# First experts' results stored by slot and gathered back in pairs of row tiles, in batch order; second experts' weights loaded between those stores

## The chip, the cores and the metric

The kernel runs on one core of a Trainium2 chip. The metric is the device time of one execution in microseconds (us). TensorE does the matmuls and transposes, VectorE and ScalarE the element-wise work and the copies out of PSUM, GpSimd (POOL in the profile) some element-wise work and all indirect DMAs, and SyncE (SP) only issues DMAs.

## The reference

An embedding of 8 batches, each of 64 image patches and 128 text tokens, so 8 x 192 = 1536 rows of 192 numbers, goes through two layers. Only the last three steps bear on the change:

```python
h = h + L0_ffn(layernorm(h))   # 8 experts, top 2, hidden 288, gelu
h = h + L1_attn(layernorm(h))
h = h + L1_ffn(layernorm(h))   # 8 experts, top 2, hidden 768, silu; output
# L1_attn: linear attention, 12 heads of 16, per batch:
k_, q_ = relu(k) + 0.25, relu(q) + 0.25
kv, k_sum = sum_n k_[n] v[n]^T, sum_n k_[n]
out = ((q_ kv) / (q_ k_sum + 1e-6)) @ proj_w.T + proj_b
```

In L0_ffn a row's result is the sum of two experts' results, each times its gate.

## The kernel before

**Tiles.** The 1536 rows are 12 row tiles of 128. Tiles 0 to 3 hold the patches of two batches each, tiles 4 to 11 the text of one batch each. The two batches of index i are `trio(i)`: patch tile i and text tiles 4 + 2i and 5 + 2i. There are four trios, and six pairs of neighbouring tiles.

**Experts.** A routing step ranks the 2 x 1536 (row, expert) entries by expert, so that each expert's rows fill whole tiles of 128 slots: 31 tiles in all. `slot` numbers are kept per entry (`sli`), and per slot the row to fetch (`idxs`) and the place of the result (`idx2`). `expert_dma` (L731) is GpSimd's program. It gathers tile i + 7's rows by an indirect DMA (L738), into a ring of 4 buffers, then stores tile i's result by another (L746). `experts` (TensorE L1903, VectorE L1529, ScalarE L1019) transposes a gathered tile, makes the hidden layer (L1941), transposes it, makes the result (L1983), and VectorE copies it (`evac_y`, L1571) into a ring of 8 buffers. The first experts' results go to `ybuf` in HBM: one row for each (choice, row), and spare rows for slots without an entry.

**Sum.** When all stores have landed, `load_acc` (L545) reads `ybuf` back with plain DMAs, the first choices' results on SP's queue into `xn`, the second choices' on ScalarE's into `a1`, each in four groups of row tiles (`ACC`). SP then issues the second experts' weights, 9.2 MB. VectorE adds each group into `h`, times the gate, and takes its statistics (`ln_start`, `ln_end`). ScalarE normalises (`ln_norm`, L834).

**Attention.** TensorE transposes the rows by neighbouring pairs (`t_pair`, L1839). `kv_mms` (L2218) makes keys and values of two pairs in four PSUM banks, `q_mms` (L2247) the queries of two pairs, `sums` (L2270) the key-value sums of a trio, `numden` (L2293) its numerators and denominators, `t_att` (L2322) and `out_proj` (L2330) the projected result. VectorE copies keys (L1642) and queries (L1650) out, masks the sums (`state`), divides (`ratio`, L1678), and adds the result to `h` (`add_att`). ScalarE copies the transposed rows (L1088), the values (L1098) and the transposed attention (L1118). Each engine's order is written out by hand. `keep_busy` (L1799) puts matmuls whose result nobody reads into a wait.

After it come the second routing and the second experts, whose results GpSimd adds into `out`.

Of the kernel before, what the change touches and what calls it, by code (L numbers as in the profile page):

```python
# [28 lines left out]
ALU = mybir.AluOpType  # L29
# [36 lines left out]
YRING = 8  # L66
NV = 2
# [23 lines left out]
LANDED = [16 * (sum(1 for n in range(NT) if n % YRING == (i - 1) % YRING) + (i - 1) // YRING + 1) if i else 16  # L91
# [7 lines left out]
def build(nc, x, out):  # L99
    ctx = ExitStack()  # L100
    with ctx:
# [26 lines left out]
        ybuf = nc.dram_tensor("expert_rows", [TOPK * NTOK + 32 * P, D], F32, kind="Internal").ap()  # L128
# [213 lines left out]

        psum = ctx.enter_context(nc.psum_tensor("bank", [P, 8 * 512], F32))
# [37 lines left out]
        route_done = sem("route_done"); idx2_ready = sem("idx2_ready"); land_ready = sem("land_ready"); turn_come = sem("turn_come")  # L381
# [5 lines left out]
        acc_ld = [sem(f"acc_ld{g}") for g in range(4)]  # L387
# [10 lines left out]
        NPAIR = NJ // 2  # L398
        NBP = B // 2
# [21 lines left out]
        PR_BANK = [(4, 7), (4, 7), (4, 7), (0, 1)]  # L421
# [32 lines left out]
        def ln_cols(n, g):  # L454
            if n == 3:
                return slice(*ACC[g])
# [96 lines left out]


        @block.sync
        def _(sp):
# [49 lines left out]
            load_acc(sp, 0)  # L606

            for e in range(NE):
# [9 lines left out]
            sp.wait_ge(xn5_ready, NJ)  # L618
            sp.dma_start(tok_rows(xd[1][:, 0:D]), xn[:, :, :]).then_inc(xd_written, 16)
# [1859 lines left out]
```

## Time and profile before

| | |
|---|---|
| time, median of 3 runs | 462.23 us (457.75 to 463.28) |
| profiled execution: its time | 462.79 us |
| profiled execution: its span | 461.0 us |
| mean granted TensorE clock | 0.956 of full speed |
| busy share of the span: TensorE matmul | 91% |
| weight load (PEld) | 71% |
| VectorE | 63% |
| GpSimd | 49% |
| ScalarE | 43% |

The span runs from the first to the last instruction that the profile shows of the core, and the execution's time is 1.8 us more. A busy share is a mean over stages that have different limits. Times in rows are us from the start of the span. "<-" before a name is what released the engine from the wait.

### The profile page before, as it was taken

Reading aid. Unit: us, or ns where it says so; the run is one execution under the profiler, and the core shown is the slowest. Engines: PE = TensorE matmul, PEld = TensorE weight load, DVE = VectorE, ACT = ScalarE, POOL = GpSimd, SP = SyncE. Lnnn points to the kernel's source line nnn. Section 1 sums busy time; section 2 is a strip of 40 time slices with the busy share of each in tenths; the row PEclk is TensorE's granted clock in tenths of the full one; section 3 lists DMA queues with packets and bytes.
Section 4 is the critical chain, followed back from the end, with each engine's and each line's share of the span. In section 5 each row is a group of like instructions: output and inputs, shape, how many; then the busy total and the mean of one; then the engine's idle time right before and its main releaser. Section 6 shows DMA issues by size and latency. Waiting matters only on the chain.

```text
span 461.0 us, 10231 instructions
## 1 busy us (share of the span) xinstructions
PE 420.2 (91%) x3568; PEld 326.3 (71%) x3568; DVE 292.3 (63%) x1360; ACT 197.3 (43%) x374; POOL 225.6 (49%) x266
## 2 busy tenths in 40 slices
PE   7999998989788988989987988977999999999993
PEld 5653655637536877878844557933999999999993
DVE  6579999999782433333558336887465566556651
ACT  1287945441751111110123401546566566566660
POOL 4302798797035666666520000334456665665544
PEclk9799799999989999898979999998999999999998
DMA  8609400010132122222169999079233233333322
GB/s 233 96 1 227 113 0 3 1 35 1 58 102 70 60 61 70 69 70 70 47 195 236 224 225 217 15 137 139 50 62 50 54 62 63 51 55 61 51 25 27
DMA packets 40128, 39.02 MB, mean 85 GB/s; under 512 B 7575, under 2 KB 37259, under 8 KB 40079
## 3 DMA queue, kind: packets, MB, share of 16 engines
q1 hardware_dynamic: 28861, 23.05, 22.5%
q0 software_dynamic: 9312, 14.03, 15.3%
q10 hardware_dynamic: 1906, 1.30, 1.0%
q8 instruction: 29, 0.48, 0.4%
q14 instruction: 20, 0.16, 0.1%
HBM read 28.00 MB, written 11.06 MB: 85 GB/s over the span
## 4 chain that ended last, share of the span: by engine, by line
PE 66%; DVE 11%; DMA 10%; ACT 4%; POOL 4%; issue 4%; POOLq 1%; SPq 0%; DVEq 0%; another core or an unknown queue 0%; ACTq 0%
PE bank L1955 11%; PE bank L1990 10%; PE bank L1941 7%; PE bank L1983 7%; DMA out<-a,idx 5%; PE bank L2036 4%; POOL reg L707 3%; PE bank L1803 3%; PE bank L1964 2%; DMA xn<-expert_rows 2%; PE bank L1918 2%; ACT xn L834 2%; DMA reg<-xn_rows,idxs 1%; PE bank L2229 1%; DMA reg<-in_patchT 1%
## 5 line engine op out<-in xcount | busy, mean ns | idle before, releaser
L738 POOL DMA_INDIRECT reg<-xn_rows,idxs x62 | 60.5, 976 | 30.3 <-issue 16.6
L1955 PE MATMUL bank<-reg,xT 64*128 64x128 f32 x1116 | 72.6, 275 | 1.4 <-issue 1.1
L758 POOL DMA_INDIRECT out<-a,idx x31 | 50.3, 1622 | 46.7 <-DMA out<-a,idx 35.8
L1955 PEld LDWEIGHTS bank<-reg,xT 64*128 64x128 f32 x1116 | 68.6, 188 | 1.5 <-issue 1.0
L1990 PE MATMUL bank<-reg 64*128 64x192 f32 x744 | 69.0, 323 | 0.0
L1990 PEld LDWEIGHTS bank<-reg 64*128 64x128 f32 x744 | 63.4, 187 | 0.0
L1803 PE MATMUL bank<-con 128*128 128x512 bf16 x201 | 55.3, 435 | 0.0
L1045 ACT ACTIVATE reg<-reg 128x1152 f32 x31 | 36.1, 1163 | 30.8 <-PE bank L1990 30.8
L1574 DVE TENSOR_SCALAR a<-bank,gs 128x192 f32<-128x192 f32 x31 | 13.0, 418 | 53.2 <-PE bank L1990 53.2
L1024 ACT ACTIVATE reg<-bank 128x288 f32<-128x288 f32 x31 | 12.5, 410 | 77.4 <-PE bank L1941 62.9
L746 POOL DMA_INDIRECT expert_rows<-a,idx x31 | 30.6, 986 | 25.2 <-DVE a L1571 19.1
L1803 PEld LDWEIGHTS bank<-con 128*128 128x128 bf16 x201 | 21.6, 111 | 27.6 <-issue 12.0
L1941 PE MATMUL bank<-reg,xTs 96*128 (+1 forms) x124 | 36.7, 418 | 4.8 <-DVE xTs L1537 4.7
L1983 PE MATMUL bank<-reg 96*128 x186 | 36.9, 336 | 0.3 <-issue 0.3
L1571 DVE COPY a<-bank 128x192 f32<-128x192 f32 x31 | 11.0, 354 | 39.6 <-PE bank L1983 20.6
L1983 PEld LDWEIGHTS bank<-reg 96*128 96x128 f32 x186 | 32.8, 195 | 3.7 <-issue 0.8
L1547 DVE TENSOR_SCALAR reg<-bank,gb 128x128 f32<-128x128 f32 x93 | 32.3, 403 | 0.0
L787 POOL TENSOR_SCALAR onep<-rs 128x3 f32<-128x3 f32 x4 | 0.9, 228 | 57.2 <-DVE nm L1189 57.2
L1941 PEld LDWEIGHTS bank<-reg,xTs 96*128 96x128 f32 (+1 forms) x124 | 21.8, 196 | 9.8 <-issue 6.2
L707 POOL TENSOR_TENSOR reg<-reg 128x128 f32<-128x128 f32 x63 | 26.1, 457 | 5.1 <-PE bank L2110 4.9
L1028 ACT ACTIVATE reg<-bank 128x384 f32<-128x384 f32 x31 | 15.2, 490 | 21.7 <-PE bank L1955 13.4
L1309 DVE TENSOR_REDUCE bank<-reg 128x6 f32<-128x24 f32 x176 | 23.9, 181 | 0.0
(363 smaller groups left out, 800.9 us busy)
## 6 DMA issues: line engine op xcount, KB each, us to landing
reg<-in_w2b SPq DMA_DIRECT2D x8, 576.0 KB, 10.2
reg<-in_w1b SPq DMA_DIRECT2D x8, 288.0 KB, 10.4
reg<-in_w1a SPq DMA_DIRECT2D x8, 216.0 KB
reg<-in_w2a SPq DMA_DIRECT2D x8, 216.0 KB
xn_rows<-xn SPq DMA_DIRECT2D x4, 384.0 KB, 2.7
reg<-in_w1b SPq DMA_DIRECT2D x8, 192.0 KB, 8.5
xn_rows<-xn SPq DMA_DIRECT2D x1, 1152.0 KB, 7.8
out<-h SPq DMA_DIRECT2D x1, 1152.0 KB
```

The costliest lines, as they stand in the source:

```text
L707: ins = nc.gpsimd.tensor_tensor(term[b % 2][k][:, 0:n, :, r, :], second[:, :, :, r, k:k + 1].to_broadcast([P, n, NCH, 4]), first[:, :, :, ...
L738: pool.indirect_dma_start(xs[:, i % RING, 0:(D, D2)[l]], None, xd[l], bass.IndirectOffsetOnAxis(ap=idxs[:, i:i + 1], axis=0)).then_inc(xs_ ...
L746: pool.indirect_dma_start(ybuf, bass.IndirectOffsetOnAxis(ap=idx2[:, i:i + 1], axis=0), ys[:, i % YRING, :], None).then_inc(scat[i % YRING ...
L758: pool.indirect_dma_start(out, bass.IndirectOffsetOnAxis(ap=idx2[:, i:i + 1], axis=0), ys[:, i % YRING, :], None, compute_op=ALU.add).then ...
L1045: nc.scalar.activation(w2r[:, p, :], w2b.rearrange("p e c n -> p (e c n)")[:, bass.ds(e * W2R, W2R)], ACT.Copy).then_inc(w2r_act, 1)
L1309: V.tensor_reduce(slot(t)[:, ch, 0:3], entries[:, ch], AX, ALU.add).then_inc(scan_self[half], 1)
L1547: ins = V.tensor_scalar(dst[:, k], src[:, :, 64 * k:64 * k + 64], gb2[:, 0, k:k + 1], gb2[:, 1, k:k + 1], ALU.mult, ALU.add)
L1803: MM(bank[bk][:, :], con[:, 0:P // 2].bitcast(BF16), con[:, 0:2 * P].bitcast(BF16), start=True, stop=True)
L1941: ins = MM(bank[2 + p][:, 0:hid], xTs[0:r, p, k, :], w1v[0:r, bass.ds(e * (NK * hid) + k * hid, hid)], start=(k == 0), stop=(k == NK - 1))
L1955: ins = MM(bank[2 + 2 * p + a][:, c * P:(c + 1) * P], w1r[rs, p, col:col + hc], xT64[rs, p, k, :], start=(c == 0 and k == 0), stop=(c == n ...
L1983: ins = MM(bank[6 + p][:, 0:D], hTs[0:r, p, c * P:(c + 1) * P], w2v[0:r, bass.ds(e * (nhc * D) + c * D, D)], start=(c == 0), stop=(c == nh ...
L1990: ins = MM(bank[Y_BANKS[i == NT - 1][a]][:, 0:D], hT2[rs, p, c * P:(c + 1) * P], w2r[rs, p, c * D:(c + 1) * D], start=(c == 0), stop=(c == ...
```

## The change

The first experts' result of tile i is stored by a plain DMA of SP, in slot order: row 128 i + p of `ybuf` is slot p of tile i. GpSimd only gathers in that stage (`first_dma`). Between those stores SP loads the second experts' weights, one expert after every third tile from tile 3 on. When all stores have landed, GpSimd fetches each row's two results by `sli`: 24 indirect gathers of 128 rows (`results_back`), by pairs of row tiles in batch order (`ORDER`: patch tile and two text tiles of each trio). VectorE adds and normalises by such pairs (`rows_back`), and `h`, `xn`, keys, values and queries are handled by pairs in that order, on every engine. The keys and values of one pair have two PSUM banks in place of four for two pairs, and queries are made for two, two, one and one pairs. The rows for the second gather are written by 12 DMAs in place of 2. The diff, cut to its core (a "..." line stands where lines are left out):

```diff
+SCAT0 = NA // YRING
...
-        ybuf = nc.dram_tensor("expert_rows", [TOPK * NTOK + 32 * P, D], F32, kind="Internal").ap()
+        ybuf = nc.dram_tensor("expert_rows", [NT * P, D], F32, kind="Internal").ap()
...
-        PR_BANK = [(4, 7), (4, 7), (4, 7), (0, 1)]
+        ND_BANK = [(6, 7), (6, 7), (6, 7), (2, 3)]
+        PR_BANK = [(6, 7), (6, 7), (6, 7), (4, 5)]
...
-        ACC = ((0, 2), (2, 4), (4, 8), (8, 12))
-        GROUPS[3] = [list(range(*ab)) for ab in ACC]
-        LN_BASE = {1: 0, 2: 3, 3: 5, 4: 5 + len(ACC)}
+        ORDER = [j for i in range(NBP) for j in trio(i)]
+        GROUPS[3] = [ORDER[2 * n:2 * n + 2] for n in range(NPAIR)]
...
-        def wait_scatters(eng, l):
+        def wait_results(eng, done):
             for s in range(YRING):
-                eng.wait_ge(scat[s], 16 * (sum(1 for i in range(NT) if i % YRING == s) * (l + 1)))
-        def load_acc(eng, p):
-            wait_scatters(eng, 0)
-            buf = (xn, a1)[p]
-            rows = tok_rows(ybuf, p * NTOK)
-            for g, ab in enumerate(ACC):
-                js = slice(*ab)
-                eng.dma_start(buf[:, js, :], rows[:, js, :]).then_inc(acc_ld[g], 16)
+                eng.wait_ge(done[s], 16 * (sum(1 for i in range(NT) if i % YRING == s) + (0 if done is y_st else SCAT0)))
         @block.sync
...
-            load_acc(sp, 0)
-            for e in range(NE):
+            def load_expert(e):
...
                 sp.dma_start(w2b[:, e, :, :], x["w2b"][e].rearrange("(c p) n -> p c n", p=HC1)).then_inc(ld_ffn1, 16)
+            for i in range(NT):
+                sp.wait_ge(y_ev, i + 1)
+                sp.dma_start(ybuf[i * P:(i + 1) * P, :], ys[:, i % YRING, :]).then_inc(y_st[i % YRING], 16)
+                if 3 <= i < 27 and i % 3 == 0:
+                    load_expert(i // 3 - 1)
...
+            for i0, i1 in ((0, NBP - 1), (NBP - 1, NBP)):
+                sp.wait_ge(xn5_ready, 3 * i1)
+                of = xn[:, 3 * i0:3 * i1, :].rearrange("p (i v) n -> p i v n", v=3)
+                pat = slice(i0, i1)
+                for c, n in ((slice(0, D), D), (slice(D, DX), DX - D)):
+                    sp.dma_start(tok_rows(xd[1])[:, pat, c], of[:, :, 0, 0:n]).then_inc(xd_written, 16)
+                    for a in range(2):
+                        sp.dma_start(tok_rows(xd[1])[:, NPJ + 2 * i0 + a:NPJ + 2 * i1:2, c],
+                                     of[:, :, 1 + a, 0:n]).then_inc(xd_written, 16)
...
+            def first_dma():
+                rows_written(0)
+                for i in range(NT):
+                    gather(0, i)
+            def results_back(n):
+                for q in (2 * n, 2 * n + 1):
+                    for k, buf in enumerate((xn, a1)):
+                        a, g = k * NJ + ORDER[q], 2 * q + k
+                        if g >= YRING:
+                            pool.wait_ge(scat[g % YRING], 16 * (g // YRING))
+                        pool.indirect_dma_start(buf[:, q, :], None, ybuf,
+                                                bass.IndirectOffsetOnAxis(ap=sli[:, 0, a:a + 1], axis=0)
+                                                ).then_inc(scat[g % YRING], 16)
...
             route_share(0)
-            expert_dma(0)
-            wait_scatters(pool, 0)
+            first_dma()
+            wait_results(pool, y_st)
+            results_back(0)
             link(nc.gpsimd.memset(vb[:, :, KC:KV], 1.0))
+            results_back(1)
             nc.gpsimd.memset(attT[KC:KC + 1, 1, :], 1.0).then_inc(att_ones, 1)
+            for n in range(2, NPAIR):
+                results_back(n)
...
-                    nc.scalar.activation(xn[:, j, :], src[:, j, :], ACT.Identity,
+                    nc.scalar.activation(xn[:, i, :], src[:, j, :], ACT.Identity,
...
-            for q in range(2):
-                ln_std(3, q)
-                ln_norm(3, q, h)
-                xt3_evac(q)
-            for g in range(1, 3):
-                ln_std(3, g + 1)
-                ln_norm(3, g + 1, h)
-                v_evac(g - 1)
-                xt3_evac(2 * g)
-                xt3_evac(2 * g + 1)
...
+            def rows3(n):
+                ln_norm(3, n, h)
+                xt3_evac(n)
...
+            ln_std(3, 0)
+            rows3(0)
+            ln_std(3, 1)
+            v_evac(0)
+            rows3(1)
+            ln_std(3, 2)
+            v_evac(1)
+            rows3(2)
+            ln_std(3, 3)
             v_evac(2)
...
+            rows3(3)
+            ln_std(3, 4)
+            v_evac(3)
             att_evac(0)
+            rows3(4)
+            ln_std(3, 5)
+            v_evac(4)
+            rows3(5)
             att_evac(1)
             ln_std(4, 0)
             norm5(0)
...
-                        dve.wait_ge(scat[s], 16 * turns(l, i, YRING))
+                        dve.wait_ge((y_st, scat)[l][s], 16 * (turns(0, i, YRING) + l * SCAT0))
...
-            for g, ab in enumerate(ACC):
-                dve.wait_ge(acc_ld[g], 16 * 2)
+            def rows_back(n):
+                for g in range(4 * n, 4 * n + 4):
+                    dve.wait_ge(scat[g % YRING], 16 * (g // YRING + 1))
                 for k, y in ((0, xn), (1, a1)):
-                    for j in range(*ab):
-                        ins = V.scalar_tensor_tensor(out=h[:, j, :], in0=y[:, j, :], scalar=gate[:, k, j:j + 1],
+                    for q in (2 * n, 2 * n + 1):
+                        j = ORDER[q]
+                        ins = V.scalar_tensor_tensor(out=h[:, j, :], in0=y[:, q, :], scalar=gate[:, k, j:j + 1],
                                                      in1=h[:, j, :], op0=ALU.mult, op1=ALU.add)
...
+            def q_evac(c):
+                first, r = Q_PAIRS[c]
+                dve.wait_ge(q_mm, c + 1)
...
+            def before_att(i0, i1, pairs):
+                dve.wait_ge(l3_ev, pairs)
...
-            for g in range(2):
-                k_evac(g)
-                if g == 0:
-                    ln_end(3, 3)
-                q_evac(g)
+            rows_back(0)
+            ln_end(3, 0)
+            rows_back(1)
+            k_evac(0)
+            ln_end(3, 1)
+            rows_back(2)
+            k_evac(1)
+            ln_end(3, 2)
+            q_evac(0)
             state(0)
+            rows_back(3)
             k_evac(2)
+            ln_end(3, 3)
             ratio(0)
+            rows_back(4)
+            k_evac(3)
+            ln_end(3, 4)
+            q_evac(1)
+            before_att(0, 2, 3)
             state(1)
+            rows_back(5)
+            add_att(0)
+            k_evac(4)
+            ln_end(3, 5)
+            ratio(1)
+            ln_end(4, 0)
             q_evac(2)
-            ratio(1)
             state(2)
-            before_att()
-            add_att(0)
+            k_evac(5)
+            add_att(1)
             ratio(2)
+            before_att(2, 4, 6)
+            q_evac(3)
             state(3)
-            ln_end(4, 0)
-            add_att(1)
             ratio(3)
             ln_end(4, 1)
             shift(0, 2)
...
             keep_busy(18, 6)
-            t_pair(3, 0)
-            def kv_mms(g):
...
+            def rows_t(n, attended):
+                pe.wait_ge(xn_ready, 2 * NJ + 2 * n + 2)
+                pe.wait_ge(xT_ready, XT_BASE[3] + n - 1)
+                if attended:
...
+            def kv_mms(n):
+                pe.wait_ge(xT_ready, XT_BASE[3] + n + 1)
+                if n:
+                    pe.wait_ge(k_ev, n)
+                    pe.wait_ge(v_ev, n)
+                for a in range(2):
...
+            def q_mms(c):
+                first, r = Q_PAIRS[c]
+                pairs = slice(first, first + r)
+                if c:
+                    pe.wait_ge(st_ev, c)
...
             def sums(i):
                 pe.wait_ge(att_ones, 1)
-                pe.wait_ge(k_ev, 2 * (1 + i // 2) + 2)
-                pe.wait_ge(v_ev, 2 * (1 + i // 2) + 2)
-                if i == 0:
-                    pe.wait_ge(xT_ready, XT_BASE[3] + NPAIR)
-                else:
-                    pe.wait_ge(st_ev, i)
+                pairs = (3 * i + 2) // 2 + 1
+                pe.wait_ge(k_ev, pairs)
+                pe.wait_ge(v_ev, pairs)
+                pe.wait_ge(q_ev, 2 * i + 2)
...
                 pe.wait_ge(st_ev, i + 1)
-                pe.wait_ge(q_ev, 2 * (1 + i // 2) + 2)
                 if i == 0:
-                    pe.wait_ge(k_ev, 6)
-                    pe.wait_ge(v_ev, 6)
+                    pe.wait_ge(rwg_ready, 1)
+                elif i < NBP - 1:
+                    pe.wait_ge(h_ready, 2 + 2 * i)
                 else:
-                    pe.wait_ge(att_ready, 2 * i)
+                    pe.wait_ge(k_ev, NPAIR)
...
             def t_att(i):
                 pe.wait_ge(att_ready, 2 * i + 2)
-                if i == 0:
-                    pe.wait_ge(q_ev, 6)
-                else:
+                pe.wait_ge(xT_ready, XT_BASE[3] + min(NPAIR, 4 + 2 * i))
+                if i:
                     pe.wait_ge(at_ev, 2 * i)
...
             def out_proj(i):
                 pe.wait_ge(at_ev, 2 * i + 2)
-                if 0 < i < NBP - 1:
-                    pe.wait_ge(h_ready, 2 + 2 * i)
+                if i == 0:
+                    pe.wait_ge(rwg_ready, 1)
...
-            for g in range(2):
-                kv_mms(g)
-                if g == 0:
-                    q_mms(0)
-                t_pair(3, 2 * g + 2)
-                t_pair(3, 2 * g + 3)
-                if g:
-                    q_mms(g)
+            rows_t(0, 0)
+            kv_mms(0)
+            keep_busy(4, 6)
+            rows_t(1, 0)
+            kv_mms(1)
+            q_mms(0)
+            rows_t(2, 0)
             sums(0)
             kv_mms(2)
             numden(0)
+            rows_t(3, 0)
+            kv_mms(3)
+            t_att(0)
+            q_mms(1)
             sums(1)
+            out_proj(0)
+            rows_t(4, 1)
+            kv_mms(4)
+            numden(1)
             q_mms(2)
-            t_att(0)
-            numden(1)
+            rows_t(5, 1)
+            t_att(1)
             sums(2)
-            out_proj(0)
-            t_att(1)
+            kv_mms(5)
+            out_proj(1)
+            q_mms(3)
             numden(2)
             sums(3)
-            out_proj(1)
             t_att(2)
             numden(3)
             out_proj(2)
...
```

## Rows read from the trace of the kernel before

**Rows 1.** Stretch, length, busy PE, PEld, DVE, ACT, POOL, clock, DMA share, GB/s
```profile
142.31:230.49 88.18, 82.84 (x461) 71.77 (x461) 35.91 (x91) 12.50 (x31) 55.07 (x58) 0.96 0.21 64
...
241.97:298.62 56.65, 50.33 (x327) 35.59 (x328) 35.15 (x137) 18.81 (x51) 3.39 (x8) 1.00 0.87 187
...
250.00:260.00 10.00, 8.91 (x42) 4.57 (x41) 6.03 (x21) 6.26 (x17) 0.00 (x0) 1.00 1.10 226
```

**Rows 2.** Chain of waits, first experts: start us, duration us, what
```profile
154.84 0.97 PE bank L1941 x4
...
157.35 0.97 PE bank L1941 x4
...
224.92 0.97 PE bank L1941 x4
```

**Rows 3.** Timelines, first experts: start, duration, engine, line, [idle before, releaser]
```profile
146.38 0.94 POOL L738 DMA_INDIRECT reg<-xn_rows,idxs  x1 [0.30 <-issue]
...
148.89 0.42 DVE L1537 COPY xTs<-bank 96x256 f32<-96x256 f32 x1 [2.33 <-remote]
...
177.80 1.14 PE L1983 MATMUL bank<-reg 96*128 x6
...
180.53 0.97 POOL L738 DMA_INDIRECT reg<-xn_rows,idxs  x1 [0.30 <-issue]
...
182.94 0.36 DVE L1571 COPY a<-bank 128x192 f32<-128x192 f32 x1 [3.77 <-PE bank L1983]
...
225.27 0.97 POOL L746 DMA_INDIRECT expert_rows<-a,idx  x1 [1.53 <-DVE a L1571]
```

**Rows 4.** Timeline, from the first experts to the attention
```profile
230.53 0.36 DVE L1571 COPY a<-bank 128x192 f32<-128x192 f32 x1 [0.64 <-PE bank L1983]
...
234.01 0.22 POOL L781 MEMSET reg<- 128x144 f32 x1 [1.60 <-DMA expert_rows<-a,idx]
...
237.41 0.75 DVE L1630 SCALAR_TENSOR_TENSOR h<-xn,gate,h 128x192 f32<-128x192 f32 x2 [0.85 <-DMA a<-expert_rows]
```

**Rows 5.** DMA issues: queue, count, KB each, median us to landing
```profile
xn_rows<-a SPq DMA_DIRECT2D x2, 96.0 KB, 1.7
...
xn<-in_table,ids POOLq DMA_INDIRECT x8, 4.7
```

**Rows 6.** Chain of waits, the first gather of the second experts
```profile
317.70 2.94 DMA reg<-xn_rows,idxs
```

**Rows 7.** Groups by line, 230 to 300 us: busy, mean ns | idle
```profile
L1854 PE MATMUL bank<-con,xn 128*128 128x128 f32 x18 | 2.8, 285 | 2.0 <-ACT xn L834 1.8
...
L2229 PE MATMUL bank<-reg 128*128 128x392 f32 x24 | 9.5, 517 | 1.7 <-ACT reg L1088 1.7
...
L2305 PE MATMUL bank<-reg 96*64 96x102 f32 x32 | 2.3, 263 | 1.4 <-ACT reg L1098 1.4
...
L2317 PE MATMUL bank<-con,a 128*96 128x128 f32 x16 | 2.9, 273 | 1.5 <-DVE reg L1650 1.5
```

**Rows 8.** The same view and stretch, VectorE and ScalarE
```profile
L1642 DVE TENSOR_SCALAR reg<-bank 128x384 f32<-128x384 f32 x6 | 3.3, 556 | 5.8 <-PE bank L2235 5.8
...
L1650 DVE TENSOR_SCALAR reg<-bank 96x512 f32<-96x512 f32 x6 | 3.8, 681 | 5.0 <-PE bank L2266 5.0
...
L1177 DVE BATCH_NORM_STATS2 st<-h 128x6 f32<-128x192 f32 x21 | 6.2, 349 | 0.2
...
L1678 DVE TENSOR_TENSOR a<-bank,z 128x192 f32<-128x192 f32 (+1 forms) x8 | 3.3, 452 | 0.1
...
L834 ACT ACTIVATE xn<-h,nmr,rstd 128x192 f32<-128x192 f32 x12 | 5.7, 536 | 4.8 <-DVE nmr L1197 4.8
...
L1098 ACT ACTIVATE reg<-bank 128x384 f32<-128x384 f32 x6 | 2.9, 487 | 0.0
...
L1088 ACT ACTIVATE reg<-bank 128x384 f32<-128x384 f32 x6 | 2.7, 500 | 1.3 <-PE bank L1854 1.3
...
L1118 ACT ACTIVATE reg<-bank 96x512 f32<-96x512 f32 x4 | 2.3, 587 | 13.3 <-PE bank L2319 13.3
```

More of the change, by code:

```diff
@@ L88 @@
 NCONST = NCON0 + 2 * P
-LANDED = [16 * (sum(1 for n in range(NT) if n % YRING == (i - 1) % YRING) + (i - 1) // YRING + 1) if i else 16
+LANDED = [16 * (SCAT0 + (i - 1) // YRING + 1) if i else 16
           for i in range(32)]
@@ L386, in build @@
         th_mm = sem("th_mm"); th_ev = sem("th_ev"); g2_mm = sem("g2_mm"); y_ev = sem("y_ev")
-        acc_ld = [sem(f"acc_ld{g}") for g in range(4)]
+        y_st = [sem(f"y_st{s}") for s in range(YRING)]
         att_ones = sem("att_ones"); base1_ready = sem("base1_ready"); pr_read = sem("pr_read")
@@ L1081, in _ @@
             experts(0, ACT.Gelu, HID0)
-            load_acc(act, 1)
             def xt3_evac(q):
@@ L1128, in _ @@
             norm5(0)
+            v_evac(5)
             att_evac(2)
@@ L1506, in route @@
                     dve.sem_inc(route_done, 1)
-                    link(V.tensor_scalar(pad, slot_v, 0.0, None, ALU.is_equal))
-                    link(V.tensor_tensor(pad, pad, con[:, C_PADQ:C_PADQ + 32], ALU.mult))
-                    V.scalar_tensor_tensor(out=idx2[:, :], in0=slot_v, scalar=-1.0, in1=pad, op0=ALU.add,
-                                           op1=ALU.add).then_inc(idx2_ready, 1)
                 else:
@@ L1631, in _ @@
                                                      in1=h[:, j, :], op0=ALU.mult, op1=ALU.add)
                     link(ins)
-                    if g and k == 0:
-                        ln_end(3, g - 1)
-                ln_start(3, g, h)
-            def k_evac(g):
-                for r in range(2):
-                    dve.wait_ge(kv_mm, 2 * g + r + 1)
-                    q = 2 * g + r
-                    V.tensor_scalar(kb[:, 2 * q:2 * q + 2, :], two_banks[1 + r][:, :, 0:D],
-                                    0.0, float(HD) ** -0.5, ALU.max, ALU.add).then_inc(k_ev, 1)
@@ L1645, in q_evac, with k_evac @@
-            def q_evac(g):
-                dve.wait_ge(q_mm, g + 1)
-                qv = qT[:, :, 512 * g:512 * g + 512].rearrange("p m (r a t) -> p m r a t", r=2, a=2)
+                ln_start(3, n, h)
+            def k_evac(n):
+                dve.wait_ge(kv_mm, n + 1)
+                V.tensor_scalar(kb[:, 2 * n:2 * n + 2, :], two_banks[1][:, :, 0:D],
+                                0.0, float(HD) ** -0.5, ALU.max, ALU.add).then_inc(k_ev, 1)
+            def q_evac(c):
+                first, r = Q_PAIRS[c]
+                dve.wait_ge(q_mm, c + 1)
+                qv = qT[:, :, 256 * first:256 * (first + r)].rearrange("p m (r a t) -> p m r a t", r=r, a=2)
@@ L1668, in ratio @@
                 dve.wait_ge(nd_mm, i + 1)
[L1669 to L1670 removed]
+                b0, b1 = (bank[n] for n in ND_BANK[i])
+                txt = b0[:, 0:4 * KV].rearrange("p (a n) -> p a n", a=4)
+                pat = b1[:, 0:2 * KV].rearrange("p (a n) -> p a n", a=2)
                 hg = KC // HD
@@ L1850, in t_pair @@
                     pe.wait_ge(xT_ready, m + q - 1)
-                if n == 3:
-                    two = xn[:, 2 * q:2 * q + 2, :].rearrange("p j n -> p (j n)")
-                    for v in range(3):
-                        ins = nc.tensor.transpose(bank[q % 2][:, v * P:(v + 1) * P], two[:, v * P:(v + 1) * P], ident)
-                    ins.then_inc(xt_psum, 1)
-                    return
                 for k in range(NK):
@@ new lines, in kv_mms @@
+            def kv_mms(n):
[4 more added lines that the diff above has]
+                for a in range(2):
+                    MM(bank[2 + a][:, 0:WKV], xT3[:, n, 2 * a * P:(2 * a + 1) * P], qkvw[:, a, D:D + WKV],
+                       start=True, stop=False)
+                for a in range(2):
+                    rs = slice(64 * a, 64 * a + 64)
+                    ins = MM(bank[2 + a][:, 0:WKV], xT3[rs, n, P:2 * P], qkvw[rs, 2, D:D + WKV],
+                             start=False, stop=True)
+                ins.then_inc(kv_mm, 1)
@@ L2265, in q_mms @@
                         rs = slice(64 * a, 64 * a + 64)
-                        ins = MM(bank[6 + a][0:KC, half(m)], qkvw[rs, 2, m * KC:(m + 1) * KC],
-                                 xT3[rs, 2 * g:2 * g + 2, P:2 * P], start=False, stop=(m == 1))
+                        ins = MM(bank[4 + a][0:KC, half(m)], qkvw[rs, 2, m * KC:(m + 1) * KC],
+                                 xT3[rs, pairs, P:2 * P], start=False, stop=(m == 1))
                 ins.then_inc(q_mm, 1)
```

197 lines of the change are left out of this document (80 added, 117 removed).

## The prediction

> **What bounds the kernel now.** I read the chain of waits first, then the timelines of the first experts, then the queue of matmuls in the attention. TensorE is the bound nearly everywhere, but not evenly. [rows 1] has the two stages that the change touches: 88.2 us of first experts and 56.7 us of attention. The second experts run outside of both and are left as they are.
>
> In the first experts the chain passes from one tile's first product (L1941) to the next in 157.35 − 154.84 = 2.51 us when nothing disturbs it [rows 2]. Between tile 6's (154.84) and tile 30's (224.92) lie 24 tiles and 70.1 us, so 70.1 − 24 × 2.51 = 9.9 us are lost. [rows 3] shows how, in one of six like events: the matmuls of 177.80 had ended at 178.94, yet VectorE copied their result only at 182.94, 3.77 us idle. That copy came 1.44 us after GpSimd's last DMA issue had ended (180.53 + 0.97). The same holds at 170.90, 194.96, 207.00 and 219.06 (1.45 us each), and at 148.89, before any result was stored: the last gather of a run that began at 137.54 ended at 146.38 + 0.94, 1.57 us earlier. After 220, when GpSimd has only stores left and rests before each (1.53 us idle at 225.27), no copy is late. So I read it thus: when GpSimd issues DMAs back to back for 6 us or longer, TensorE's signals to VectorE and ScalarE arrive late, by up to 4 us, until GpSimd rests. A gather and a store cost it 0.97 + 0.99 us and two gaps of 0.30, 2.56 us, more than TensorE's 2.51 us: it never rests of itself.
>
> Then the hand-over: last result copied at 230.89, last store landed before 234.01, first sum of h at 237.41 [rows 4], first transposes of the attention at 241.97, where the second window of [rows 1] begins. From there to the end of the last output projection (298.62, that window's end) TensorE waits 2.0 + 1.7 + 1.4 + 1.5 = 6.6 us [rows 7].
>
> **The change, part by part.** The profiled execution has a span of 461.0 us and took 462.79 us; the median of the three runs is 462.23, 0.6 us below. I sum differences and set them on the median.
>
> *First experts, the store moved from GpSimd's queue to SP's.* GpSimd keeps 1.28 us of gather in each 2.51 us. It rests in each tile, so the late signals go: −9.9 us. The rest, up to the first 8 gathers back to back, stays. The price of a store on SP: 96 KB from SBUF land 1.7 us after their issue [rows 5]; 8 result buffers give 8 tiles, 20 us, so it is hidden. The index arithmetic taken out of the routing (three small VectorE steps) lay beside the first gather's 3 us: nothing.
>
> *Weights of the second experts, one expert per three tiles, on the same SP queue.* One expert is 1.15 MB; at the 226 GB/s of the third window of [rows 1] that is 5.1 us of each 7.5 us. Behind it a store waits at most 5.1 us, and the ring covers 20. A gather has 4 buffers, issued as its predecessor of four tiles before is transposed: 10 us of notice, against 4.7 us to landing for gathers beside the patches' load [rows 5] and 2.94 us alone [rows 6]. Hidden; if that cover is gone, every gather is late and TensorE waits (a rival). I add 0.5 us for the zero fill of 0.67 MB, which SP now issues just ahead of the first gathers back. Bounds: 0 and the 3 us that it takes at 226 GB/s.
>
> *Hand-over.* Before: 237.41 − 230.89 = 6.5 us from the last copy to the first sum. After: store 1.8, then four indirect gathers for pair 0; three intervals of 1.28, and 2.94 from the fourth's issue to landing [rows 6], and 0.1 of signals: 8.7 us. +2.2.
>
> *Attention, by pairs.* The products are the same, so TensorE's own work is 56.65 − 6.6 = 50 us. What differs is where it waits. One pair of key and value banks in place of two pairs, and program orders by pair, put more hand-overs on the path. With the durations of [rows 8] and the orders written in the diff:
> - after five of six transposes it waits for the copy of xT: 0.50 + 0.1 each, 3.0;
> - transposes of pair 1: key copy 0.56, value copy 0.57, norm of two tiles 0.98, 0.1 of signals, less 0.9 of fillers: 1.3; the 0.9 of fillers are extra too;
> - sums(0) and sums(1) now wait for the query copy, 2 × 0.68 less overlap, 1.3 and 0.1 of signals, the first with 0.55 of transposes over it: 0.8 + 1.4 = 2.2;
> - transposes of pair 3: after sums(0) come state 0.64, rows_back(3) 2.47 (four sums in 1.5, statistics in 0.9), key copy 0.56, value copy 0.57, norm 0.98, in all 5.2, over which only kv_mms(2) and numden(0) lie, about 3.9 of the stage's 50 us of matmuls: 1.4;
> - sums(2): q_evac(2) stands on VectorE behind ln_end(4, 0), which waits on ScalarE's attention copy (0.86) and roots 0.5; with ln_end 0.36 and query copy 0.8: 2.6;
> - sums(3): ratio(2) 1.5 (0.82 of it the two products at L1678), before_att 0.55, query copy 0.8, 0.1 of signals: 3.0.
>
> Together 13.5 + 0.9 = 14.4 us against 6.6: +7.8. The gathers are not among these waits: they are issued in 24 × 1.28 = 31 us and two memsets (1.6), so pairs 1 to 5 land about 5.4, 12, 17, 22 and 27 us after pair 0. Only pairs 1 and 2 are waited for; rows_back(3) comes 20 us after the first sum.
>
> *Late signals under that burst.* 24 gathers back to back are just the run in which signals came late in [rows 3]. Memsets break it after 8. Between its 6th us and its end some 6 to 8 signals of TensorE are on the path. None late: 0. Each late by one issue interval of 1.3 us: 9. TensorE sends about one signal in 2 us there, against four in 2.5 us in the experts, so I take the lower part: +2.
>
> Not on the path: the rows written for the second gather, now 12 smaller DMAs in place of 2. SP needs about 0.45 us for each, 2.6 us for the last six, and the routing behind them takes over 10 us.
>
> **Sum:** −9.9 + 0.5 + 2.2 + 7.8 + 2.0 = +2.6 us. On the median: 464.8, say 465; on the profiled execution 465.4.
>
> GpSimd's issues in [rows 3] took 0.94 to 0.99 us whether VectorE copied beside them or not. The Trainium skill, SBUF — State Buffer, "Who interferes with whom", says that a VectorE instruction with two SBUF inputs and a GpSimd instruction that reads SBUF block one another for a whole instruction. The 24 sums of h have two SBUF inputs and now run beside GpSimd's gathers, which speaks against the change; by it the gathers of a pair would land up to 1.6 us later and the sum would be about +4 (an estimate by that page). No row of before has the two side by side.
>
> **Rivals.**
> *A. The hand-over waits mostly overlap (faster).* TensorE's waits in the attention stay at 6.6 us and no signal is late. For it: all six of my waits are laid end to end from averages, and the old order had such waits too, only 6.6 us of them. Against: three of them are plain program order. 462.2 − 9.9 + 0.5 + 2.2 = 455.0, and up to 3 us below if pair-wise starts overlap still better.
> *B. Late signals under the gather burst (slower).* Place: TensorE to VectorE and ScalarE, from the first to the fourth pair. Price: seven to nine signals at 1.3 us, 10 us in place of 2. It decides from about 1.2 us a signal on, where the sum passes +9. For it: [rows 3]. Against: fewer signals per us. 473.
> *C. The stalls of the first experts stay (the change does not do what it moves the store for).* Either the lateness does not come from GpSimd's queue, or weights delay the gathers as much as it did. Then −9.9 is missing: 475. For it: a correlation only. Against: all seven events end 1.1 to 1.6 us after the end of GpSimd's last issue.
>
> The copies that GpSimd's gathers have to share with the weights are seen in [rows 5]: 4.7 us to landing in place of 2.94. The Trainium skill, DMA: Bandwidth & Descriptors, "Issuing engines are not separate DMA queues", says that all queues run on the same 16 DMA engines and interleave; the row agrees, and it is what rival C would act by.
>
> **How the numbers follow.** Forecast 0.45, A 0.27, B 0.16, C 0.12. A change under 2%, 9.2 us, is about what a measurement of this kernel cannot tell from none. Faster by over 2% (below 453.0): half of A, 0.14. Slower (above 471.5): C, two thirds of B and 0.04 of the forecast, 0.27. Within: 0.59. The forecast's own range is 459 to 471. The range for 8 in 10 goes to A's middle and to B and C: 453 to 476.
>
> **What would show it.** In the first experts: tiles at 2.51 us throughout, no copy idle over 1.5 us, last copy near 221. Stores on SP landing within 7 us. First sum of h about 8.7 us after the last copy, gathers 1.28 us apart. In the attention: first transposes near 234, waits of TensorE of some 14 us, the last output projection ending near 301. Signals: compare the end of a matmul group with the start of the copy that waits for it, inside and after the burst. I am wrong if the experts' stage still takes over 84 us (C), or if the attention from first transposes takes under 60 us (A) or over 72 (B).

## The result: slower by 4.1%

The changed kernel took 478.42 us (median of 6, 476.50 to 483.19) against 461.0 us of the kernel before on the same chip (median of 11), ratio 1.041 (1.036 to 1.046). A first comparison gave 479.15 us (median of 4, 473.89 to 483.0) against 460.46, ratio 1.037 (1.024 to 1.049). Both lie above my range of 453 to 476.

The first profiled execution (483.0 us, span 481.0) belongs to a disturbed run that the first ratio leaves out, so I read the second one (476.50 us, span 474.4) and give the first beside it. The page of the second, its busy shares, and then stretches in the columns of [rows 1]: the first experts, the attention from its first transposes to the last output projection, and four times 4 us inside it.

```profile
span 474.4 us, 10330 instructions
...
PE 424.2 (89%) x3600; PEld 328.4 (69%) x3600; DVE 292.7 (62%) x1364; ACT 198.0 (42%) x376; POOL 218.2 (46%) x259
```

```profile
141.00:216.90 75.90, 74.97 (x450) 66.95 (x448) 35.04 (x91) 13.38 (x31) 23.78 (x26) 1.00 0.75 197
230.24:312.50 82.26, 59.88 (x348) 40.51 (x348) 38.66 (x149) 19.41 (x53) 19.38 (x25) 0.88 0.07 21
244.00:248.00 4.00, 1.90 (x13) 0.89 (x11) 0.00 (x0) 0.56 (x2) 3.09 (x4) 1.00 0.29 81
248.00:252.00 4.00, 0.00 (x0) 0.00 (x0) 0.00 (x0) 0.00 (x0) 2.35 (x3) 0.76 0.30 86
252.00:256.00 4.00, 1.02 (x6) 1.05 (x7) 1.28 (x2) 0.49 (x1) 0.00 (x0) 0.50 0.02 5
256.00:260.00 4.00, 4.00 (x16) 2.27 (x15) 2.33 (x8) 0.00 (x0) 0.00 (x0) 0.50 0.01 2
```

The first row answers to the first of [rows 1]: TensorE is busy for 74.97 of 75.90 us at full clock, where it was 82.84 of 88.18. The second answers to the second of [rows 1]: 82.26 us in place of 56.65. From 248 to 252 TensorE and the two copying engines do nothing at all, while GpSimd issues; and then 4.00 us of full work are done at a clock of 0.50, which is 1.2 GHz.

Where each stretch begins, from the timelines (first gather, last result copied, first sum of h):

```profile
133.85 1.06 POOL L743 DMA_INDIRECT reg<-xn_rows,idxs  x1 [3.90 <-DVEq L1536]
...
216.54 0.36 DVE L1597 COPY a<-bank 128x192 f32<-128x192 f32 x1 [0.64 <-PE bank L2013]
...
225.87 0.75 DVE L1659 SCALAR_TENSOR_TENSOR h<-xn,gate,h 128x192 f32<-128x192 f32 x2 [3.85 <-DMA a<-expert_rows,sli]
```

With the first gather of the kernel before at 137.54 and [rows 4]:

| stretch, us | before | changed | difference | first profile of it |
|---|---|---|---|---|
| up to the first gather | 137.5 | 133.9 | -3.7 | 135.2 |
| first gather to last copy | 93.4 | 83.1 | -10.3 | 83.1 |
| last copy to first sum of h | 6.5 | 9.0 | +2.5 | 9.1 |
| first sum to last output projection | 61.2 | 86.6 | +25.4 | 92.1 |
| from there to the end of the span | 162.4 | 161.9 | -0.5 | 161.5 |

The first line is not the change: no step of it lies there, and the same stretch took 132.2 to 137.7 us in the other kernels below. The fourth holds the loss. In it a timeline of TensorE, VectorE, ScalarE and GpSimd reads:

```profile
244.32 1.11 PE L2292 MATMUL bank<-reg 64*96 64x256 f32 x8
245.35 0.55 PE L2257 MATMUL bank<-con,xn 128*128 128x128 f32 x3
...
250.01 0.94 POOL L766 DMA_INDIRECT a<-expert_rows,sli  x1 [0.30 <-issue]
...
253.54 1.28 DVE L1676 TENSOR_SCALAR reg<-bank 96x512 f32<-96x512 f32 x2 [10.18 <-remote]
253.59 0.49 ACT L1112 ACTIVATE reg<-bank 128x384 f32<-128x384 f32 x1 [9.04 <-remote]
...
254.98 1.64 PE L2306 MATMUL bank<-reg 128*96 128x102 f32 x8 [9.08 <-DVE reg L1676]
```

The queries (L2292) are ready at 245.42, but VectorE's copy of them (L1676) starts at 253.54, 8.1 us later and 2.6 us after the last of the 24 gathers had been issued (250.95). The next pair's transposes (L2257) are ready at 245.90, and ScalarE's copy of them (L1112) starts at 253.59: two signals are held, and both come at the same time. TensorE waits for 9.08 us. In the first profile the same wait is 8.98 us and ends 2.75 us after the last issue.

### The profile page after: what moved, and what is told of

Read it like the earlier page. It is cut to its first block, busy times and chain, and to the rows that moved or that the text cites. A ratio compares the mean times of both kernels' runs of the same rounds, so it can differ in the third digit from the quotient of the medians.

```text
span 481.0 us, 10330 instructions
## 1 busy us (share of the span) xinstructions
PE 432.0 (90%) x3600; PEld 335.2 (70%) x3600; DVE 292.6 (61%) x1364; ACT 198.2 (41%) x376; POOL 217.9 (45%) x259
## 4 chain that ended last, share of the span: by engine, by line
PE 52%; DMA 22%; DVE 8%; issue 6%; ACT 5%; POOL 3%; another core or an unknown queue 2%; POOLq 1%; SPq 0%; DVEq 0%; ACTq 0%
DMA out<-a,idx 20%; PE bank L1971 7%; PE bank L2013 6%; PE bank L1839 5%; PE bank L2066 4%; POOL reg L714 3%; PE bank L2363 3%; PE bank L1994 2%; PE bank L2267 2%; PE bank L1985 2%; ACT xn L859 2%; PE bank L1948 1%; PE bank L2020 1%; PE bank L1854 1%
## 5 line engine op out<-in xcount | busy, mean ns | idle before, releaser
L1839 PE MATMUL bank<-con 128*128 128x512 bf16 x217 | 58.2, 427 | 0.0
L1839 PEld LDWEIGHTS bank<-con 128*128 128x128 bf16 x217 | 23.1, 110 | 29.4 <-issue 11.9
L1971 PE MATMUL bank<-reg,xTs 96*128 (+1 forms) x124 | 35.3, 406 | 0.3 <-DVE xTs L1563 0.3
L2013 PE MATMUL bank<-reg 96*128 x186 | 35.2, 325 | 0.0
L2013 PEld LDWEIGHTS bank<-reg 96*128 96x128 f32 x186 | 31.7, 189 | 3.1
L1332 DVE TENSOR_TENSOR reg<-reg,bank 128x18 f32<-128x18 f32 x176 | 22.7, 171 | 0.1
```

Of the source, the lines that this page charges most:

```text
L1332: V.tensor_tensor(turn, turn, slot(t)[:, ch, 0:3].unsqueeze(2).to_broadcast([P, 2, 3, 3]), ALU.mult).then_inc(scan_self[half], 1)
L1839: MM(bank[bk][:, :], con[:, 0:P // 2].bitcast(BF16), con[:, 0:2 * P].bitcast(BF16), start=True, stop=True)
L1971: ins = MM(bank[2 + p][:, 0:hid], xTs[0:r, p, k, :], w1v[0:r, bass.ds(e * (NK * hid) + k * hid, hid)], start=(k == 0), stop=(k == NK - 1))
L2013: ins = MM(bank[6 + p][:, 0:D], hTs[0:r, p, c * P:(c + 1) * P], w2v[0:r, bass.ds(e * (nhc * D) + c * D, D)], start=(c == 0), stop=(c == nh ...
```

## The experiments

Twelve kernels ran. "Attention" is from here on the fourth stretch of the table. Each ratio is to the kernel before on the same chip, whose median was 462.85 us for runs 1 to 4, 461.56 for 5, 6, 7 and 9, and 460.79 for 8, 10 and 11, so times of different chips are compared by the difference to it.

**1. The change with rests for GpSimd.**

```diff
             for n in range(2, NPAIR):
+                pool.wait_ge(xn_ready, 2 * NJ + 2 * n - 2)
                 results_back(n)
```

> The changed kernel with one wait more on GpSimd: before the gathers of each pair from the third on, it waits until ScalarE has normalised the pair two before (xn_ready). So it never issues more than 4 or 8 gathers back to back. Theory L (late signals): the single wait of 9 us of TensorE for the query copy, whose release came 2.7 us after the last of 24 gathers had been issued, goes, and with it most of the low clock behind it (0.50 to 0.61 from 250 to 262 us, 0.81 over the stage): attention from first transposes to last output projection 65 to 70 us instead of 87.9, time about 458 to 463. Rival O (the order by pairs itself): the hand-overs of 13 us and the low clock that they cause stay, only the 9 us go: stage 77 to 79, time about 468.

467.53 us, ratio 1.012 (1.008 to 1.015). The long wait is gone, and attention takes 76.5 us. GpSimd's rests were 1.84, 2.32 and 4.20 us. The stretch from the first transposes, and the wait ahead of the first sums:

```profile
231.96:304.17 72.21, 57.23 (x347) 39.81 (x348) 38.59 (x149) 19.42 (x53) 19.52 (x25) 0.93 0.09 24
```

```profile
248.72 0.92 PE L2307 MATMUL bank<-reg 128*96 128x102 f32 x8 [1.00 <-DVE reg L1677]
```

The wait for the query copy is 1.00 us. Against the first profile of the change TensorE waits 15.0 us and not 22.2, and its busy time is 57.2 and not 65.6, so the slower clock goes with the wait. The time lies at rival O's 468, not at theory L's 458 to 463. The stage from the first transposes, 72.2 us, lies between the two ranges. Something else in the change costs the rest.

**2. Stores, weights and 24 gathers back, but the old order.** Its gathers, in the order of row tiles:

```diff
-            load_acc(sp, 0)
-            load_acc(act, 1)
+                for j in range(j0, j1):
+                    for k, buf in enumerate((xn, a1)):
+                        a, g = k * NJ + j, 2 * j + k
...
+                        pool.indirect_dma_start(buf[:, j, :], None, ybuf,
+                                                bass.IndirectOffsetOnAxis(ap=sli[:, 0, a:a + 1], axis=0)
+                                                ).then_inc(scat[g % YRING], 16)
```

> The kernel before with the first half of the change alone: stores by slot on SP, weights one expert per three tiles, 24 gathers back to back by row tiles in the old order (0 to 11), groups and attention orders as before. Theory L: the burst withholds TensorE's signals here too, at least one wait of 5 us or more ends only after GpSimd's last gather, and the attention stage takes 65 us or more (56.7 before); time about 460 to 468. Rival O: the order by pairs is the cause, so here the stage is back at 57 to 60 us and the time at 449 to 454 (460.5 less 12 in the experts, plus 2 or 3 at the hand-over).

470.61 us, ratio 1.015 (1.010 to 1.021), attention 79.0 us, so the stage is as long as theory L says and the time is above its 460 to 468. But the theory's own sign is missing: TensorE's longest wait, 7.53 us, ends at 247.15, and the last gather is issued at 251.61. The groups' sums come first on VectorE in this order, and wait for gathers that land one by one.

```profile
244.26 1.41 DVE L1652 SCALAR_TENSOR_TENSOR h<-xn,gate,h 128x192 f32<-128x192 f32 x4 [8.59 <-DMA a<-expert_rows,sli]
```

So this run does not tell late signals from late rows. It shows that the old order alone does not save the gathers.

**3. The stores alone.** The kernel before, with GpSimd's stores of the first experts' results moved to SP:

```diff
+            for i in range(NT):
+                sp.wait_ge(y_ev, i + 1)
+                sp.dma_start(ybuf[i * P:(i + 1) * P, :], ys[:, i % YRING, :]).then_inc(y_st[i % YRING], 16)
             load_acc(sp, 0)
```

> The kernel before with the stores of the first experts' results alone moved: SP stores them in slot order, GpSimd only gathers, then stores the last 8 tiles' results a second time into a tensor that nobody reads, one per tile, which it needs for its semaphores. The sum reads the rows back as before, in two plain loads, so rows of other tokens are added (that part of the result is not the reference's). Weights, attention and orders as before. If the late signals in the first experts came from GpSimd's gathers and stores without a rest: no copy late after tile 6, 2.51 us per tile, the stage 10 to 12 us shorter, time 449 to 452. If the gain in the changed kernel came from elsewhere (earlier weights, for one): 458 or more.

452.07 us, ratio 0.979 (0.973 to 0.985). First gather to last copy 83.2 us (before 93.4), attention 60.9 us (61.2), no copy of a result idle for 2 us where the kernel before has seven:

```profile
176.65 0.36 DVE L1584 COPY a<-bank 128x192 f32<-128x192 f32 x1 [1.35 <-PE bank L1996]
176.92 0.41 DVE L1550 COPY xTs<-bank 96x256 f32<-96x256 f32 x1
```

The whole gain in the first experts is the store that GpSimd no longer issues; SP moves the same 31 tiles of 96 KB, and no signal is late. The weights have no part in it.

**4. Rests, and matmuls in TensorE's waits.**

```diff
+                keep_busy((10, 6, 8, 10)[i], (6, 6, 6, 0)[i])
                 pairs = (3 * i + 2) // 2 + 1
```

> The kernel with GpSimd's waits (as in the run with the rest) and besides 10, 6, 8 and 10 matmuls whose result nobody reads ahead of the four sums, where TensorE otherwise waits for the query copy. If the low clock of the attention comes from TensorE's waits there: granted clock 0.95 or more over the stage, 3 to 6 us less than with the rest alone, time about 455. If the clock is low for another reason: no less than with the rest alone, or up to 4 us more where the fillers outlast the waits.

466.48 us, ratio 1.008 (1.004 to 1.011), no less than run 1 by more than the runs scatter.

```profile
229.93:302.01 72.08, 62.39 (x377) 41.27 (x382) 38.43 (x148) 19.54 (x53) 19.41 (x25) 0.95 0.09 24
```

Busy time rose by 5.2 us and the waits fell by 5.3 (72.21 - 57.23 = 15.0, now 9.7). The clock rose from 0.93 to 0.95 only. Fillers of a fixed number buy nothing here.

**5. The order by pairs without gathers.** SP reads stored rows back with plain loads:

```diff
+            for n in range(NPAIR):
+                for k, buf in enumerate((xn, a1)):
+                    sp.dma_start(buf[:, 2 * n:2 * n + 2, :],
+                                 ybuf[k * NTOK + 2 * n * P:k * NTOK + 2 * (n + 1) * P, :].rearrange("(q p) n -> p q n", p=P)
+                                 ).then_inc(rb[n], 16)
```

> The changed kernel without the 24 gathers: SP reads the stored rows back by pairs with 12 plain loads (rows of other tokens, so the sum is not the reference's). GpSimd stores the last 8 tiles' results a second time, one per tile, into a tensor that nobody reads, for its semaphores. Orders, banks and groups are the changed ones. It gives the price of the order by pairs by itself, from first sum of h to last output projection (before 61.2 us, changed 92.1, with rests 76.5). If the order and its 13 us of hand-overs is the price that the rests did not take away: 72 to 76 us, time 462 to 466. If the pace of the gathers (a pair in 5 us) is: 62 to 66 us, time about 453.

468.44 us, ratio 1.016 (1.010 to 1.023), attention 76.2 us, 15.0 more than before with no gather in it.

```profile
231.78:300.89 69.11, 55.67 (x347) 39.27 (x347) 36.08 (x141) 19.32 (x53) 3.42 (x8) 0.95 0.02 8
276.00:280.00 4.00, 4.00 (x19) 2.29 (x18) 0.64 (x2) 0.00 (x0) 1.37 (x3) 0.66 0.02 6
288.00:292.00 4.00, 3.03 (x19) 2.66 (x20) 1.16 (x4) 0.00 (x0) 0.00 (x0) 0.62 0.00 0
```

Three parts. TensorE waits 69.1 - 55.7 = 13.4 us (before 56.65 - 50.33 = 6.3), so +7.1. Its busy time is 5.3 longer: about 3.4 in two stretches of lower clock behind long waits (the groups from 275.07 take 1.42, 1.00 and 2.25 us, the same ones at full clock 0.87, 0.60 and 1.58), 1.0 for four fillers more, 0.5 for queries in four groups of matmuls in place of three (9.6 us, before 9.1), and 0.4 not assigned. And the first transposes come 7.1 us after the first sum (before 4.6), +2.5. The last part belongs to this run and not to the changed kernel: its first two tiles are normalised at 228.90, 2.9 us before the 30 fillers of the hand-over let the transposes start, while the changed kernel has its first transposes 4.4 us after the first sum. So the order by pairs by itself costs 69.11 - 56.65 = 12.5 us. The longest waits are for the query copies:

```profile
275.07 1.42 PE L2321 MATMUL bank<-reg 128*96 128x102 f32 x8 [2.57 <-DVE reg L1691]
...
288.97 1.65 PE L2321 MATMUL bank<-reg 128*96 128x102 f32 x8 [3.22 <-DVE reg L1691]
```

**6. The same, with the 24 gathers into buffers that nobody reads.**

```diff
-                        pool.indirect_dma_start(buf[:, q, :], None, ybuf,
+                        pool.indirect_dma_start(spare[:, g % 3, :], None, ybuf,
```

> Plain loads by pairs as in the run beside it, and the 24 gathers back to back as well, but into three spare buffers that nobody reads: nothing in the attention waits for them (except the fillers of TensorE for the fourth). If signals are late for GpSimd's issues alone: one or more waits of TensorE of 4 to 10 us that end within 3 us of the last gather's issue, and 8 us or more over the run without the gathers, 472 or more. If the wait in the changed kernel came through its data: within 2 us of the run without them.

479.64 us (476.77 to 485.41), ratio 1.033 (1.027 to 1.039): over run 5 on the same chip 11.2 us by the medians, 7.7 us by the two ratios. VectorE, ScalarE and GpSimd:

```profile
249.74 1.29 DVE L1684 TENSOR_SCALAR reg<-bank 96x512 f32<-96x512 f32 x2 [4.50 <-remote]
...
252.60 0.49 ACT L1121 ACTIVATE reg<-bank 128x384 f32<-128x384 f32 x1 [6.16 <-remote]
...
259.75 0.64 DVE L1695 TENSOR_TENSOR reg<-bank,con 96x204 f32<-96x204 f32 x2 [8.73 <-remote]
```

```profile
256.03 0.95 POOL L775 DMA_INDIRECT reg<-expert_rows,sli  x1 [0.30 <-issue]
```

TensorE waits 3.39 and 2.86 us at these two, not 4 to 10 as expected; the second ends 2.8 us after the last issue. Transposed rows that were ready at 247.78 reached ScalarE at 252.60, and the queries of the first wait were ready at 247.30: these two signals came through in the middle of the run of issues, 2.4 and 4.8 us late. The price is there with no data waited for, so it is the gathers themselves and not the rows that they bring. Whether GpSimd's issue or the transfer behind it holds the signals, this run does not tell: it has both.

**7. A memset between the gathers.**

```diff
+                if n > 2:
+                    link(nc.gpsimd.memset(spare[:, 0, :], 0.0))
                 results_back(n)
```

> The changed kernel with a memset of 0.3 us on GpSimd, and the wait for its end, ahead of the gathers of pairs 3, 4 and 5, in place of rests. If any instruction between the gathers lets TensorE's signals through, the long wait goes and the time is that of the run with rests, 467. If GpSimd has to be idle for a microsecond or so, the wait stays: one of over 5 us, time 474 to 480.

476.46 us, ratio 1.029 (1.022 to 1.036). The long wait is still there, so another instruction of 0.27 us between does not do. Here the two signals are held longest: the queries, ready at 243.07, are copied at 251.54, 8.5 us later, and the transposes, ready at 243.55, at 253.65, 10.1 us later. The last issue ends at 251.38.

```profile
251.54 1.28 DVE L1680 TENSOR_SCALAR reg<-bank 96x512 f32<-96x512 f32 x2 [10.54 <-remote]
...
253.65 0.49 ACT L1116 ACTIVATE reg<-bank 128x384 f32<-128x384 f32 x1 [11.45 <-remote]
```

**8. Memsets in place of the gathers.** Run 5 with this:

```diff
+            for n in range(40):
+                link(nc.gpsimd.memset(spare[:, :, :], 0.0))
```

> The changed order with plain loads by pairs (rows of other tokens, so the sum is not the reference's) and, in place of the 24 gathers, 40 memsets of 128 x 576 on GpSimd into a buffer that nobody reads, each waiting for the one before, about 30 us. If late signals come from GpSimd being busy or writing SBUF at all: a wait of over 4 us as with the 24 gathers, 476 or more. If they come from its DMA issues: no late signal, the time of the plain loads alone, 468.

469.61 us, ratio 1.015 (1.009 to 1.021), as run 5 (1.016). 25 us of memsets leave TensorE's waits and busy time where they were; no wait of VectorE, ScalarE or TensorE in the attention shows "remote".

```profile
234.95:304.06 69.11, 55.67 (x347) 39.33 (x347) 36.09 (x140) 19.31 (x53) 17.82 (x33) 0.95 0.03 9
```

**9. A version meant to be faster.** SP's stores and gathers by neighbouring pairs, VectorE and ScalarE pair by pair, TensorE's order the old one:

```diff
+            k_evac(0)
+            rows_back(3)
+            ln_end(3, 3)
+            q_evac(0)
+            rows_back(4)
...
```

> A version meant to be faster: stores by slot on SP, weights between them, gathers back by neighbouring pairs with GpSimd's rests, VectorE and ScalarE take them pair by pair, but banks and TensorE's order are the old ones (keys of two pairs in four banks, all six pairs transposed before the first sums). If the order by pairs costs 10 us or more, this gets most of it back: first sum to last output projection 64 to 69 us, time 455 to 459, below the kernel before. If the pace of the gathers sets the time: 74 or more, 466.

468.26 us, ratio 1.014 (1.008 to 1.020), attention 78.4 us. A miss. Though GpSimd had rested, for 1.21 us up to 242.19, ScalarE got the rows that had been transposed by 242.85 only at 248.49, 1.5 us after the next four issues (246.96), and TensorE stood still for 7.78 us.

```profile
242.19 0.94 POOL L794 DMA_INDIRECT xn<-expert_rows,sli  x1 [1.21 <-ACT xn L857]
...
248.49 0.49 ACT L1110 ACTIVATE reg<-bank 128x384 f32<-128x384 f32 x1 [5.67 <-remote]
```

**10 and 11. Rests in the kernel before.** After every third, or every fifth, store of the first experts GpSimd waits until it has landed:

```diff
                     scatter(i)
+                    if l == 0 and i % 3 == 2:
+                        pool.wait_ge(scat[i % YRING], 16 * (i // YRING + 1))
```

> The kernel before, with rests: after every third store of a first experts' result GpSimd waits until that store has landed, some 1.2 us. Gathers and stores then take it (3 x 2.56 + 1.2) / 3 = 2.96 us a tile at most, 31 tiles in 92. Theory L: with no run of issues over 7.7 us hardly a signal of TensorE comes late: late updates over 2 us at most 3 (22 before), and the stage is set by GpSimd instead, 88 to 92 us against 93.3. Time 457 to 462. Rival (the stalls have another cause): late updates as many as before and the rests on top, 466 or more.

> The same with a rest after every fifth store: runs of issues of 12.8 us. Theory L with the onset as in the kernel before (signals late from some 6 us of issues on): late signals in each run, stalls that end with each rest, about six of them, stage 90 to 94, time 459 to 463. If a rest of 1.2 us in 14 is enough: GpSimd's (5 x 2.56 + 1.2) / 5 = 2.8 us a tile, stage 87, time 455 to 457.

461.20 us, ratio 0.998 (0.994 to 1.002), and 466.54 us, ratio 1.015 (1.007 to 1.023). First gather to last copy 92.9 and 96.4 us. With rests after every third store seven copies still come after 2.07 to 4.61 us idle, as many as before. A rest here is 1.61 us or more without an issue, and six of the seven copies start inside one, 1.08 to 1.37 us after the last issue has ended, for example:

```profile
161.53 0.36 DVE L1573 COPY a<-bank 128x192 f32<-128x192 f32 x1 [3.06 <-remote]
...
161.87 0.97 POOL L738 DMA_INDIRECT reg<-xn_rows,idxs  x1 [1.61 <-DMA expert_rows<-a,idx]
```

So such a rest does let a signal through, but the six issues up to the next rest hold the next one, and the rests cost what they save. My expectation of three late signals at most was wrong, and so was that of 459 to 463 us for the rests after every fifth store.

**12. The changed kernel again**, the second profile above.

> The changed kernel once more, for a second profile and an interval over more rounds. Theory L: the long wait again begins after the sixth us or later of the last run of gathers and ends within 3 us of the end of the last of them, 9 to 10 us; attention from first transposes to last output projection 82 to 88 us; time 474 to 480, 3 to 4% over the kernel before. If the long wait was chance of one execution: below 470 and a stage near that with rests, 72.

The long wait came again, attention from first transposes 82.3 us.

## Why the prediction was wrong

**Stalls in the first experts, -9.9: right.** -10.3 measured, and run 3 shows that the store alone brings it (rival C falls). 2.5 us a tile is seen throughout, no copy idle over 1.5 us, last copy at 216.90.

**Weights and zero fill, +0.5: no sign of a cost.** First gather to last copy is 83.1 us with the weights between the stores and 83.2 without (run 3).

**Hand-over, +2.2: right,** +2.5. Gathers went out 1.25 us apart. The last copy at 216.90, where I had named 221, owes 3.7 us to the stretch ahead of the change.

**Attention by pairs, +7.8: the waits right, the size too small.** TensorE's waits, summed step by step to 13.5 and 0.9 of fillers, were 13.4 and 1.0 in run 5, and the four waits for the query copy, 0.8, 1.4, 2.6 and 3.0 in the sum, were 1.00, 1.48, 2.57 and 3.22. But the sum let all else run at the full clock of the second of [rows 1]; the lower clock behind the waits, at nothing in the sum, cost about 3.4 us more, and the term measured 12.5. Rival A, that the waits overlap, falls with the same row.

**Late signals, +2.0: the step that failed.** I let six to eight signals on the path be late by a fraction of an issue each, after the 1.3 us of one interval, and named ten as the dear case (rival B, 473). What happened is that two signals, of the queries and of the next transposes, were held back at once, for 8.1 and 7.7 us, until GpSimd's run of issues was over. [rows 3] had it: there a copy was late by up to 4 us, "until GpSimd rests", in a kernel where GpSimd had to rest soon since it waited for that very copy. Here nothing that GpSimd needs hangs on TensorE, so it goes on to its last gather. The rule I had read, I did not apply to a run with no such end. By the times the term is 17.4 - 4.7 = 12.7 us (the changed kernel and run 1, each over the kernel before on its chip), or 7.7 to 11.2 us (run 6 over run 5). In the profiles, against run 1, it is 7.4 us of waits and 2.7 us of slower work (59.88 less 57.23) in the second, 7.2 and 8.4 us in the first. Rival B had the right cause, place and sign, but it priced seven to nine short delays where there were two long ones at once, and had no term for the clock; that its 10 us lie so near is in part luck.

**The sum by what the runs showed:** -10.3 + 2.5 + 12.5 (order, run 5) + 13.2 (gathers beside it, 82.26 less 69.11; 10.1 of them go with the rests of run 1, 3.1 do not) - 0.2 (first sum to first transposes) = +17.7. The medians differ by 478.4 - 461.0 = 17.4, but the two profiled spans only by 13.4: the sum leaves out the -3.7 and -0.5 of the first and the last stretch, and that these are scatter is my reading.

**Sums of h beside gathers.** By the Trainium skill, SBUF — State Buffer, "Who interferes with whom", VectorE's sums with two SBUF inputs and a GpSimd instruction that reads SBUF would block one another. The trace shows next to nothing of it: two sums took 0.75 us each as in [rows 4], and the issues beside them mostly 0.95 us (1.14 at most) where [rows 3] has 0.94 to 0.97, so the extra time that I had worked out from the page did not come. Whether the issue of a gather is such an instruction no run here shows.

**What stays open.** Whether it is GpSimd's issues or the transfers behind them that hold the signals. How long a run of issues is safe: after rests of 1.84 us and more, runs of four issues held nothing (run 1), and run 4 with two rests of 1.19 and 0.98 us had no late signal either; runs of six issues between rests of 1.61 us held signals (run 10), and so did one of four issues after a rest of 1.21 us (run 9). And why TensorE's signals are the late ones: in run 6 VectorE's signal of 251.03 released TensorE at 251.17, while one of TensorE to ScalarE was held from 247.78 to 252.60. No version of mine that computes the reference is faster than the kernel before; run 3 shows that 2.1% lie in the first experts for a read-back that costs no more than the two plain loads.

## What to carry to other kernels

In this kernel GpSimd's indirect DMAs, back to back, held up the signals of another engine; ask what would make the issuing engine rest, and if nothing does, price the case that the wait lasts to the end of the run. A long wait of TensorE costs more than its length, 7 us of waits here 2.7 to 8.4 us more, since the work behind it runs at a lower clock: put a clock term beside it. And cost a moved stage as a whole: the 10 us won in the first experts were real, but the read-back that they needed came with an order that cost 12.5 and with gathers that cost 13.2 beside it.

## What the runs showed of the hardware

- With GpSimd's indirect DMAs 1.25 us apart, signals of TensorE to VectorE or ScalarE were held for up to 10.1 us (run 7). Most came 1.1 to 2.8 us after an issue that no other followed at once; one came 0.2 us after it (run 7), and two in the middle of the run of issues (run 6). 25 us of memsets on GpSimd held nothing up (run 8).
- TensorE stood without work from 245.90 to 254.98. It was granted 0.76 from 248 to 252 and 0.50 (1.2 GHz) from 252 to 260, so for some 5 us of work after the wait; from 256 to 260 it was busy all the time.
- 31 stores of 96 KB and 9.2 MB of weights on one queue, with the gathers 197 GB/s over 76 us, delayed the gathers so little that TensorE waited 0.6 us for them in the whole stage.
